# Four of eight batches by hats and matmuls in all sixteen units, their extra inputs loaded by a piece of their own

## What is computed

```python
off = einsum('bwkc,ock->bow', xr, w_off) + b_off
dy, dx = off[:, 0::2], off[:, 1::2]
px = base + dx                       # a position for each tap of each window
x0 = floor(px); frac = px - x0
v0, v1 = x[x0], x[x0 + 1]            # two neighbours, 0 outside of x
wy = max(0, 1 - abs(dy))
val = wy * ((1 - frac) * v0 + frac * v1)
out = einsum('bckw,dck->bwd', val, w_def) + b_def
```

## Time and profile before

| what | us |
|---|---|
| median of 3 runs | 809.06 |
| lowest and highest | 805.83, 812.85 |
| span of the one profiled execution | 1468.2 |

### The profile page before, as it was taken

One profiled execution on the slowest core, in us unless ns is written; L12 is line 12 of the kernel. 1 busy time (PEld: TensorE's weight loads), 2 busy tenths in 40 slices (PEclk: granted clock), 3 DMA queues, 4 the chain that ended last, 5 costly groups with the idle time before them and its releaser, 6 DMA issues. The chain is left out here.

```text
span 1468.2 us, 18721 instructions
## 1 busy us (share of the span) xinstructions
PE 862.4 (59%) x7080; PEld 475.2 (32%) x7080; DVE 592.0 (40%) x1409; ACT 599.1 (41%) x1048; POOL 508.6 (35%) x547
## 2 busy tenths in 40 slices
PE   2206445466739457293937729366663955829987
PEld 0103122233315234061514405133331523405653
DVE  3103242264506236081813507245450623607854
ACT  0408124253429144070806607144441923407552
POOL 5460625332450633606071260623245063260000
PEclk9957667587759668596957959678785966859999
DMA  8821414152511404216140421405251140310000
GB/s 178 188 58 35 90 24 118 30 107 61 112 38 25 108 24 85 70 46 126 46 98 15 82 72 29 108 20 107 67 115 40 27 106 24 66 47 11 10 15 11
DMA packets 115654, 96.85 MB, mean 66 GB/s; under 512 B 71180, under 2 KB 104036, under 8 KB 115564
## 3 DMA queue, kind: packets, MB, share of 16 engines
q1 hardware_dynamic: 94464, 57.55, 14.5%
q0 software_dynamic: 17104, 34.93, 13.2%
q10 hardware_dynamic: 3996, 3.17, 1.1%
HBM read 91.10 MB, written 4.48 MB: 65 GB/s over the span
## 5 line engine op out<-in xcount | busy, mean ns | idle before, releaser
L394 POOL DMA_INDIRECT G<-in_x,idx x528 | 502.8, 952 | 805.8 <-DVE idx L604 649.8
L904 PE MATMUL bank<-HT,XN 128*32 128x184 f32 x3072 | 277.5, 366 | 419.2 <-issue 384.5
L448 ACT ACTIVATE HT<-PXB,c_lneg 128x736 f32<-128x736 f32 x192 | 159.9, 897 | 522.5 <-remote 466.9
L904 PEld LDWEIGHTS bank<-HT,XN 128*32 128x32 f32 x3072 | 133.8, 121 | 570.1 <-issue 510.5
L624 DVE TENSOR_SCALAR var<-bank 94x4 f32<-94x4 f32 x32 | 4.9, 153 | 477.0 <-remote 474.9
L458 ACT ACTIVATE HT<-HT 128x2208 f32<-128x2208 f32 x80 | 163.2, 2040 | 0.9
L1026 PE MATMUL bank<-Z,c_w1e 128*128 128x376 f32 x288 | 125.8, 519 | 10.2 <-ACT HE L532 5.1
L532 ACT ACTIVATE HE<-bank,c_fb 128x376 f32<-128x376 f32 x128 | 73.0, 570 | 94.8 <-PE bank L1026 87.3
L1049 PE MATMUL bank<-GE,c_w2e 128*128 128x376 f32 x256 | 105.7, 501 | 1.8 <-DVE GE L787 1.7
L787 DVE TENSOR_TENSOR GE<-HE,bank 128x376 f32<-128x376 f32 x128 | 68.7, 537 | 67.2 <-issue 33.2
L846 PE MATMUL bank<-VT,c_wdef 128*128 128x380 f32 x256 | 88.3, 499 | 1.8 <-DVEq L696 1.8
(11 more groups left out here) (150 smaller groups left out, 1039.8 us busy)
## 6 DMA issues: line engine op xcount, KB each, us to landing
xt<-in_x SPq DMA_DIRECT2D x248, 96.0 KB, 3.2
PXB<-pw SPq DMA_DIRECT2D x16, 768.0 KB
G<-in_x,idx POOLq DMA_INDIRECT x528
XN<-in_x SPq DMA_DIRECT2D x16, 384.0 KB, 3.3
WYB<-pw SPq DMA_DIRECT2D x64, 48.0 KB
PXE<-pwx SPq DMA_DIRECT2D x4, 768.0 KB
out<-OUTS SPq DMA_DIRECT2D x64, 44.0 KB
XNE<-in_x SPq DMA_DIRECT2D x4, 384.0 KB, 4.5
```

What stands on the lines that cost most here:

```text
L394: pool.indirect_dma_start(out=G[h][:, col, :], out_offset=None, in_=x.rearrange("b (l c) -> (b l) c", c=C), in_offset=bass.IndirectOffsetO ...
L448: act.activation(HT[half][:, c, :, :].rearrange("p g (w n) -> p g w n", n=4), src.rearrange("p (g w i n) -> p i g w n", g=NG, i=2, n=4)[:, ...
L904: mm = pe.matmul(bank[0][32 * g:32 * g + 32, HW * c:HW * c + HW], rows_[:, bb, C * ch + 32 * c:C * ch + 32 * c + 32], HT[half][:, k, g, :] ...
```

## The change

FULLER holds all sixteen units. So every unit gathers two pairs only and sends four batches through hats and matmuls. The loads of XNE, PXE and WYE are taken out of load_rows and spread_positions and put in a new piece, load_extra, named z0. It works on unit s + 2 (AHEAD 2) and stands in SyncE's list behind q0, which works on unit s + 3. With all units fuller, its wait is for all four dense_out pieces of the unit ahead of it.

```diff
--- before.py
+++ after.py
@@ -11,7 +11,7 @@
 NB = 8
 GB = 6
 UNITS = B // NB
-FULLER = (0, 4, 8, 12)
+FULLER = tuple(range(UNITS))
 LP = 768
 WP = LP // K
 NG = 4
@@ -53,7 +53,7 @@
 
 
 AHEAD = {"m": 0, "e": 0, "r": -1, "f": -2, "g": -2, "d": -2, "c": 1, "b": 1, "n": 1, "h": 2, "k": 1, "a": 3, "p": 3,
-         "q": 3, "y": 3, "t": 4, "x": 4}
+         "q": 3, "y": 3, "z": 2, "t": 4, "x": 4}
 SHIFTED = {
     "tensor": {"n0": 2, "m0": 1},
     "vector": {"n0": 2, "g0": -1, "n1": 2, "m1": 1, "r7": 0, "g1": -1, "r8": 0, "m2": 1, "g2": -1, "m3": 1, "g3": -1, "m4": 1, "r10": 0, "g4": -1, "r11": 0, "n2": 2, "r12": 0, "r6": 0, "c0": 2, "c1": 2, "c2": 2, "r13": 0},
@@ -67,7 +67,7 @@
                "h1 h2 f6 h3 f7 a3 r6 a4 m0").split(),
     "vector": ("n3 g5 r14 b3 g6 r6 g7 a4 d8 r7 d9 c0 m1 r8 n0 m2 g0 c1 m3 g1 m4 r10 g2 c2 n1 g3 n2 r11 t0 g4 r12 "
                "t1 r13 t2 t3").split(),
-    "sync": ("y0 x0 p0 q0 e0 e1 e2 d9").split(),
+    "sync": ("y0 x0 p0 q0 z0 e0 e1 e2 d9").split(),
 }
 
 ORDERS = {}
@@ -307,16 +307,6 @@
                 wy = pw[bass.ds(u, 1), 0].rearrange("a (g n) -> g a n", g=NG)
                 for g in range(NG):
                     sp.dma_start(WYB[h][32 * g:32 * g + 32, :], wy[g].broadcast_to([32, WP * 8])).then_inc(wy_in[h], 16)
-                if u in FULLER:
-                    v = fuller_before(u)
-                    sp.wait_ge(pwx_out, 6 * 16 * (v + 1))
-                    if v:
-                        sp.wait_ge(dense_read, dense_before(FULLER[v - 1] + 1))
-                    sp.dma_start(PXE[:, :], pwx[v:v + 1, 1].broadcast_to([128, NG * WP * 8])).then_inc(pxx_in, 16)
-                    wy = pwx[v:v + 1, 0].rearrange("a (g n) -> g a n", g=NG)
-                    for g in range(NG):
-                        sp.dma_start(WYE[32 * g:32 * g + 32, :], wy[g].broadcast_to([32, WP * 8])).then_inc(wyx_in, 16)
-
             def load_rows(m, h):
 
                 u = 2 * m + h
@@ -324,12 +314,21 @@
                     sp.wait_ge(dense_read, dense_before(u - 1))
                 sp.dma_start(XN[h][:, :, :], x[bass.ds(NB * u + GB, 2), :].rearrange(
                     "b (p n) -> p b n", p=128)).then_inc(xn_in[h], 16)
-                if u in FULLER:
-                    v = fuller_before(u)
-                    if v:
-                        sp.wait_ge(dense_read, dense_before(FULLER[v - 1] + 1))
-                    sp.dma_start(XNE[:, :, :], x[NB * u + GB - 2:NB * u + GB, :].rearrange(
-                        "b (p n) -> p b n", p=128)).then_inc(xnx_in, 16)
+            def load_extra(m, h):
+
+                u = 2 * m + h
+                if u not in FULLER:
+                    return
+                v = fuller_before(u)
+                if v:
+                    sp.wait_ge(dense_read, dense_before(FULLER[v - 1] + 1))
+                sp.dma_start(XNE[:, :, :], x[NB * u + GB - 2:NB * u + GB, :].rearrange(
+                    "b (p n) -> p b n", p=128)).then_inc(xnx_in, 16)
+                sp.wait_ge(pwx_out, 6 * 16 * (v + 1))
+                sp.dma_start(PXE[:, :], pwx[v:v + 1, 1].broadcast_to([128, NG * WP * 8])).then_inc(pxx_in, 16)
+                wy = pwx[v:v + 1, 0].rearrange("a (g n) -> g a n", g=NG)
+                for g in range(NG):
+                    sp.dma_start(WYE[32 * g:32 * g + 32, :], wy[g].broadcast_to([32, WP * 8])).then_inc(wyx_in, 16)
 
             def write_estimate(a):
                 def piece(m, h):
@@ -357,7 +356,7 @@
             load_first(sp, (0, 2))
             for name, _s in CONSTS[NFIRST:NFIRST + 1]:
                 sp.dma_start(cs[name][:, :], consts[name]).then_inc(lneg_in, 16)
-            pieces = {"x0": next_x, "p0": write_positions, "q0": spread_positions, "y0": load_rows, "d9": store,
+            pieces = {"z0": load_extra, "x0": next_x, "p0": write_positions, "q0": spread_positions, "y0": load_rows, "d9": store,
                       "e0": write_estimate(0), "e1": write_estimate(1), "e2": read_estimate}
             steps("sync", pieces, -3, UNITS + 2)
             for h in range(2):
```

## The result

The changed kernel takes 1119.7 us (median of four runs) against 810.3 us: a ratio of 1.380, 95% interval 1.374 to 1.387. Three of the four took 1112.3 to 1120.4 us; the fourth, 1391.7 us at a mean granted clock of 0.56 where the others had 0.90, is left out of the ratio. The forecast was 999 us in 930 to 1060. The direction was right, but 309 us came on top where 190 were expected.

The account below looks back on a forecast made before the run. The stretches between gathers were taken as the timed kernel, with gathers hidden and ACT as the floor. 809.4 us, less 0 for gathers, plus 141 for hats and 49 for the PXE wait, gave 999 us, range 930 to 1060.

Parts of the forecast that it names:

- The sum: Whole kernel: 809.4 us outside the gathers, less 0 for gathers, plus 141 for hats and 49 for waits: 999 us.
- the wait for PXE: ACT's first distance pass on PXE waits for the load: 3.5 us after absorption, units 1 to 14, 49 us.
- the chain: From a step's first gather: SP's writes, PXE issue, landing at about +26 us, against k4 due at about +16.
- The upper bound: Largest total allowed for the PXE wait: 14 x 7.6 = 106 us.
- The gathers: Twelve units lose 12 gathers each, 180 us of POOL, worth nothing in the timed run; bounds 0 to 14 us.
- rival C: POOL sets the timed run before; freeing it gives slack and ACT's floor ends it, say 918 us; chance 0.10.
- The hats: Twelve units gain two batches of hats, matmuls and combine: 11.7 us a step, 141 us in all.
- The floor of 905 us: Time of the changed kernel if ACT, 802 us busy, never idled between first and last hat: 905 us.
- The calibration: Profiled span less gathers, 1468.2 - 502.8 - 156.0 = 809.4 us, taken as the timed run, median 809.06.
- B: The load of PXE is hidden anyway, so only the hats are paid: 951 us; chance 0.22.
- D: Faster: each gather taken away gives up to 1.25 us to all engines; fully true 770 us; chance 0.03.
- E: Worse: the full 9 us wait for PXE with nothing absorbed, PE starving too: 1076 us; chance 0.10.

Follow-up runs that it names:

- the kernel with two buffers: Changed kernel with XNE and WYE doubled, PXE put in an unused third of G, loaded three steps ahead: 951.5 us, ratio 1.174.
- load ahead of xt: Changed kernel with load_extra right behind load_rows in SyncE's list, ahead of xt loads, small writes and spread: 946.9 us, ratio 1.169.
- second profile of before: The kernel before, profiled once more with no edit: measured 814.6 us, span 812.8 us.

## Why the prediction was right or wrong

*The sum.* 809 + 141 + 49 was to be 999. The terms came to these: 810, then 946.9 - 810.3 = 137 for the hats in place of gathers, then 1119.7 - 946.9 = 173 for the load (168 against the kernel with two buffers). The profiles say the same by steps: 13 of them at 43.1, 51.5 and 62.6 us in before, load ahead of xt, and after.

*The step that failed* is the size of the wait for PXE: "I take 5 us of wait, 3.5 after absorption ... in units 1 to 14". Measured are 11.1 us in 15 units, with nothing absorbed. The ends of the chain were right: k4 due at +14.2 (I had +16), landing at about +25.7 (I had +26). What lies between was partly luck: PXE is asked for at +14.2, 2 us before the earliest I had and 4 before the trace's +18.4, and then takes 11.8 us to land (median) where I had some 7.6; the two errors cancel. The trace's own numbers gave 26 - 16 = 10. I then discounted them three times. I took the writes for slowed by the profiler, but PXE lands as late in a profile whose span agrees with the timed run. I cut the upper end because ACT's list is "hardly ever at its earliest", but in the step shown ACT is ready for k4 at +14.2, before the +16 that I had. And I let 1.4 us be absorbed by idle time that lies behind k4; against the kernel with the load ahead of xt the step is longer by the whole 11.1 us. I also left out unit 0, which waits too. 15 x 10 = 150 us, undiscounted, would have given 1100.

*The upper bound* of 14 x 7.6 was too low for the same reason, and the range with it.

*The gathers.* "I take nothing" for what their loss is worth fitted the sum, but its reason was wrong. The new profile shows no standstill, and POOL busy almost without a pause from unit 2 on: rival C's picture. Taking hats away instead costs 33 us. POOL set the pace before, with PE 95% busy beside it; after the change ACT sets it from a little above, and POOL waits 479.3 us. Nothing is gained from POOL as its relief overshoots: 30 us of gathers a step under 49 us of hats and the rest.

*The hats.* 11.7 us a unit, 141 in all, against 137. It came out of stretches of an odd execution; there a step with its extra lasted 55 us and one without 43. In the second profile of before these are 48.2 to 48.9 us and about 46, only 2 to 3 us apart. The 137 us are made otherwise: 13 steps at ACT's 51.5 us in place of a mean of 43.1 that POOL sets, 109 us, and 29 us more from unit 15's first gather on. So it is luck that the term agrees. ACT's busy time was right (802 forecast, 799.3 measured) and so was its role: relieved of 112 of the some 291 us of the extra passes, the step shortens until PE ends it. The floor of 905 us stands 42 below the measured 947.

*The calibration*, span less gathers equals the timed run, was a coincidence to 0.3 us. In the profile after, 1118.5 less 480 us of gathers would be 638. The forecast for the profiled span, 1430 us, fell with it; so did the thought that the gathers' stretch would cover the load.

*Rivals.* B (the load is hidden, 951) is what the kernel with the load ahead of xt does, not this one. C had the kernel before right, but its end, 918, wasn't reached: ACT holds 947. D, faster, had nothing for it. E had the right mechanism and nearly the size, 1076 us, and was given 0.10: its 14 x 9 = 126 us stood for 166 us of waits.

The rule of the Trainium skill, SBUF — State Buffer, section "SBUF: two separate sides", on VectorE holding up a gather's descriptors, shows here at a small size. In the second profile of before:

```profile
403.86 0.96 DVE L665 TENSOR_TENSOR VAL<-G 128x768 f32<-128x768 f32 x1
403.91 1.72 POOL L394 DMA_INDIRECT G<-in_x,idx  x1 [0.30 <-issue]
```

The 31 gathers that start while VectorE adds the two neighbours (VAL<-G, line 665, both inputs in SBUF) take 1.35 us on average, the other 497 take 0.95. Of the 27 gathers over 1.1 us, 24 end 0.82 us behind that pass, however early in it they began. It is this short pass that holds them, not the longer G pass that I looked at the earlier trace rows. In all it costs POOL 12.5 us there and 5 in the changed kernel; it doesn't decide between the rivals.

## What to carry to other kernels

A load for the next use into a single buffer is due when its last reader is done, not when its turn in a queue comes: here moving six DMAs ahead of the xt loads, the small writes and the spread, behind the same wait, gives back 173 us of 309 without a byte of memory. Where work is moved from one engine to others, add up each engine's step on both sides: 41 us on POOL became 30, while ACT went from an average of 37 to 50 (599.1 and 799.3 us over 16 units), so the balance was overshot. And where a profiled span and the timed runs differ by 80%, take a second profile before anything is calibrated on the first.

## What was not expected of the hardware

Twelve writes of 2 KB take SP 8.4 us to issue in the step shown (436.27 to 444.62), and their 1536 pieces of 16 bytes pass until 448.6; for as long the DMA engines move 22 to 80 GB/s, and the spread asked for at 444.75 doesn't begin before 448.2. A 768 KB spread asked for behind all that takes 11.8 us to land (median); asked for ahead of the writes it takes 8.5. A gather that starts while VectorE runs a pass with two inputs in SBUF ends 0.82 us behind that pass, up to 1.72 us in place of 0.94. The one profiled execution with a span of 1468.2 us, in which a run of gathers let PE start only some 80 instructions in 45 us, stays unexplained.
